# A conditional residual stack on one core: matrices made inside the step, and the last convolution read out in blocks of 32 partitions

## What is computed

```python
# layers 0 and 2 (each with weights of its own)
h = gelu(embedding @ W0 + b0); h = gelu(h @ W1 + b1)
att = softmax(h @ W2 + b2)                                  # 8 weights an example
agg_w = einsum('bk,koi->boi', att, weight[..., 0])          # one 128 x 128 matrix an example
x = x + einsum('boi,bih->boh', agg_w, x) + (att @ bias_k)[:, :, None]
# layers 1 and 3
x = x + conv1d(x, weight, groups=4, padding=4) + (c @ c_weight.T)[:, :, None] + bias[None, :, None]
```

## Time and profile before

| | |
|---|---|
| median of 3 runs | 2982.37 us (2981.94 to 2983.42) |
| profiled execution | 2982.91 us |
| its span, first to last instruction | 2981.1 us |
| PE busy | 2905.9 us (97%) |
| ACT, POOL, DVE busy | 1552.4, 1551.1, 1312.3 us |
| first matmul of layer 0 | at 85.75 us |
| mean granted TensorE clock | 0.985 |

### The profile page before, as it was taken

How to read it: one execution, slowest core, us unless ns; L and a number is a source line. 1 busy time by engine, 2 the same in 40 slices (tenths; PEclk the granted TensorE clock), 3 DMA queues, 4 the chain that set the end, 5 groups by cost and what they waited for, 6 DMA issues and landing times.

```text
span 2981.1 us, 121239 instructions
## 1 busy us (share of the span) xinstructions
PE 2905.9 (97%) x49252; PEld 2885.6 (97%) x49252; DVE 1312.3 (44%) x2142; ACT 1552.4 (52%) x2358; POOL 1551.1 (52%) x1796
## 2 busy tenths in 40 slices
PE   4899999999999999999999999999999999999997
PEld 2799999999999999999999999999999999999996
DVE  5344444444444444444444444444444444444441
ACT  4455555555555555555555555555555555555552
POOL 0455555555555555555555555555555555555552
PEclk7899999999999999999999999999999999999998
DMA  7465665665665665665665655655655656656653
GB/s 312 106 178 157 163 173 157 165 171 158 165 170 158 166 169 158 167 168 158 171 164 158 173 162 158 175 160 158 178 157 159 179 156 161 178 155 162 176 156 110
DMA packets 339978, 493.88 MB, mean 166 GB/s; under 512 B 59624, under 2 KB 190832, under 8 KB 322288
## 3 DMA queue, kind: packets, MB, share of 16 engines
q1 hardware_dynamic: 339952, 493.51, 60.9%
HBM read 208.06 MB, written 150.99 MB: 120 GB/s over the span
## 4 chain that ended last, share of the span: by engine, by line
PE 97%; DMA 1%; DVE 1%; ACT 0%; SPq 0%; issue 0%; POOL 0%; POOLq 0%; DVEq 0%; ACTq 0%
PE ps L317 72%; PE ps L302 24%; DMA mixed<-work 1%; DMA conv_raw<-conv_w 0%; SPq L228 0%; DVE work L558 0%; ACT work L412 0%; DVE y L542 0%; DVE y L587 0%; PE ps L279 0%; DMA work<-mix_b 0%; ACT xp L399 0%; PE ps L251 0%; POOL work L642 0%; DMA m_raw<-mixed 0%
## 5 line engine op out<-in xcount | busy, mean ns | idle before, releaser
L317 PE MATMUL ps<-y,conv_parts 32*128 32x512 f32 x36864 | 2667.9, 390 | 3.2 <-DVE y L587 3.2
L317 PEld LDWEIGHTS ps<-y,conv_parts 32*128 32x128 f32 x36864 | 2547.7, 184 | 9.1 <-DVE y L587 4.1
L587 DVE SCALAR_TENSOR_TENSOR y<-ps,bias,y 128x512 fp32r<-128x512 f32 x1536 | 1085.3, 750 | 1446.9 <-ACT y L438 1440.2
L438 ACT ACTIVATE y<-ps,bias 128x512 fp32r<-128x512 f32 x1536 | 1046.4, 690 | 683.8 <-PE ps L317 646.3
L635 POOL TENSOR_TENSOR xp<-x_t,xp 128x512 fp32r<-128x512 f32 x512 | 647.0, 1300 | 0.0
L302 PE MATMUL ps<-xp,m_parts 32*128 32x512 f32 x6144 | 621.1, 391 | 24.2 <-POOL xp L635 24.2
L628 POOL TENSOR_TENSOR m_parts<-m_raw,m_parts 128x512 fp32r<-128x512 f32 x256 | 331.7, 1296 | 585.5 <-ACT m_parts L444 585.4
L302 PE MATMUL ps<-y,m_parts 32*128 32x512 f32 x6144 | 618.9, 390 | 0.1
L302 PEld LDWEIGHTS ps<-xp,m_parts 32*128 32x128 f32 x6144 | 560.7, 184 | 25.9 <-issue 24.4
L302 PEld LDWEIGHTS ps<-y,m_parts 32*128 32x128 f32 x6144 | 562.2, 183 | 0.7 <-issue 0.5
L624 POOL COPY bias<-bias_table 128x4 f32 (+1 forms) x512 | 102.0, 200 | 816.5 <-DMA work<-work 662.5
(11 more groups left out here) (38 smaller groups left out, 37.3 us busy)
## 6 DMA issues: line engine op xcount, KB each, us to landing
x_t<-x SPq DMA_DIRECT2D x512, 256.0 KB, 5.1
work<-work SPq DMA_DIRECT2D x2048, 64.0 KB, 2.0
out<-work SPq DMA_DIRECT2D x128, 1024.0 KB, 4.8
m_raw<-mixed SPq DMA_DIRECT2D x1024, 64.0 KB, 4.4
mixed<-work SPq DMA_DIRECT2D x8, 2048.0 KB, 7.9
work<-mix_w SPq DMA_DIRECT2D x2, 2048.0 KB, 12.7
conv_raw<-conv_w SPq DMA_DIRECT2D x2, 768.0 KB, 10.8
work<-small SPq DMA_DIRECT2D x1, 852.0 KB
```

The lines of the kernel that those rows point to most:

```text
L317: ins = nc.tensor.matmul(ps[:, 4 + t, :], conv_parts[layer][rows, w, s, :], src[rows, a, p_in, q:q + N], start=(k == 0), stop=(k == CONV - 1))
L438: nc.scalar.activation(dst, src, ACT.Identity, bias=bias[layer][:, k:k + 1]).then_inc(high_set[layer], 1)
L587: nc.vector.scalar_tensor_tensor(out=dst, in0=src, scalar=bias[layer][:, k:k + 1], in1=high.bitcast(fp32), op0=ALU.add, op1=ALU.subtract). ...
```

## The change

The making of the matrices moves from the start into the step. A table of attention weights, repeated on all partitions, is built at the start (`att_table`); the 8 matrices of each mixing layer lie in SBUF with the identity as a ninth (`mix_sb`). For each example and layer a product of 128x1152 elements is made (`prod`), by DVE for layer 0 and by POOL (`scale`) for layer 2, and DVE sums it over the nine to `m_sum`. SP stores this one matrix to `scratch` and loads it back in the layout of `m_raw`.

The last convolution is read by ACT and DVE at once, in pieces of 32 partitions: phases 0 and 1 of each bank by ACT, 2 and 3 by DVE, straight to the channels and times of `o_t`. The 16 shuffle DMAs and the POOL copies are gone. Conv 1 may write a bank when both engines have read their pieces of it. The convolutions go through their shifts input phase by input phase, so that the wait for `low` 2 is one for each phase.

At the start the first weights and x(0) are loaded ahead of the rest, the gelu table is loaded early, and the bias tables are made behind the attention. The last example is stored in four parts.

```diff
+        PIECES = (("act", "act", "dve", "dve"),) * G
+        def pieces(e, g):
+            return [p for p in range(PH) if PIECES[g][p] == e]
+        def out_piece(g, p):
+            return o_t[CG * g:CG * (g + 1), :].rearrange("c (n p) -> c p n", p=PH)[:, p, :]
...
         @block.sync
...
+            def store_matrix(layer, j):
+                sp.wait_ge(summed[layer], j + 1)
+                sp.dma_start(scratch[layer // 2][bass.ds(j, 1)].rearrange("s c o -> (s c) o"), m_sum[layer][:]).then_inc(stored[layer], 16)
+            def load_matrix(layer, j, first):
+                if not first and layer == 0:
+                    sp.wait_ge(m_set[layer], j)
+                sp.wait_ge(stored[layer], 16 * (j + 1))
...
             def step(i, inner):
+                if has(i, inner, -1):
+                    load_matrix(0, i + 1, not inner and i == -1)
                 if has(i, inner, 0):
-                    if inner or i >= 1:
-                        sp.wait_ge(m_set[2], i)
-                    load_matrix(2, i)
-                if has(i, inner, 2):
-                    for g in range(G):
-                        sp.wait_ge(phases_set, nth(i - 2, g))
-                        for p in range(PH):
-                            sp.dma_start(o_ch[CG * g:CG * (g + 1), p, :], o_ph[CG * p:CG * (p + 1), g, :]).then_inc(shuffled[p], 16)
+                    load_matrix(2, i, not inner and i == 0)
+                if has(i, inner, -2):
+                    store_matrix(0, i + 2)
+                if has(i, inner, -1):
+                    store_matrix(2, i + 1)
                 if has(i, inner, -2):
                     sp.wait_ge(x_low_set, 4 * (i + 2))
                     load_x(i + 2)
-                    sp.wait_ge(m_set[0], i + 2)
-                    load_matrix(0, i + 2)
                 if has(i, inner, 2):
-                    sp.wait_ge(in_time_set, 4 * (i - 1))
-                    sp.dma_start(out[i - 2], o_t).then_inc(out_done, 16)
+                    for g in range(G):
+                        if not inner and is_last(i) or g == G - 1:
+                            for e in out_set:
+                                sp.wait_ge(out_set[e], pieces_until(e, i - 2, g))
+                        if not inner and is_last(i):
+                            sp.dma_start(out[i - 2][CG * g:CG * (g + 1)], o_t[CG * g:CG * (g + 1)]).then_inc(out_done, 16)
+                    if inner or not is_last(i):
+                        sp.dma_start(out[i - 2], o_t[:]).then_inc(out_done, 16)
...
         @block.tensor
...
                 def free1(g):
                     if before:
-                        pe.wait_ge(phases_set, nth(i - 2, g))
+                        out_read(i - 2, g)
...
         @block.scalar
...
                 if before:
                     for g in range(G):
                         act.wait_ge(mm[3], nth(i - 2, g))
                         if g == 0:
                             act.wait_ge(bias_set[3], i - 1)
                             if inner or i > 2:
-                                for p in range(PH):
-                                    act.wait_ge(shuffled[p], 16 * G * (i - 2))
-                        nc.scalar.activation(o_ph[:, g, :], ps[:, 4 + g, :], ACT.Identity,
-                                             bias=bias[3][:, g:g + 1]).then_inc(phases_set, 1)
+                                act.wait_ge(out_done, 16 * (i - 2))
+                        for p in pieces("act", g):
+                            rows = slice(CG * p, CG * (p + 1))
+                            nc.scalar.activation(out_piece(g, p), ps[rows, 4 + g, :], ACT.Identity,
+                                                 bias=bias[3][rows, g:g + 1]).then_inc(out_set["act"], 1)
...
         @block.vector
...
+            def matrix(layer, j, first):
+                l = layer // 2
+                if layer == 0:
...
+                    nc.vector.tensor_tensor(prod[layer][:], mix_sb[layer][:],
+                                            att_table[:, bass.ds(j, 1), l, :].broadcast_to([128, C, K + 1]),
+                                            ALU.mult).then_inc(scaled[layer], 1)
+                dve.wait_ge(scaled[layer], j + 1)
+                if not first:
+                    dve.wait_ge(stored[layer], 16 * j)
+                nc.vector.tensor_reduce(m_sum[layer][:], prod[layer][:], AX_X, ALU.add).then_inc(summed[layer], 1)
...
+                if has(i, inner, 2):
+                    for g in range(G):
+                        dve.wait_ge(mm[3], nth(i - 2, g))
+                        if g == 0:
+                            dve.wait_ge(bias_set[3], i - 1)
+                            if inner or i > 2:
+                                dve.wait_ge(out_done, 16 * (i - 2))
+                        for p in pieces("dve", g):
+                            rows = slice(CG * p, CG * (p + 1))
+                            nc.vector.tensor_scalar(out_piece(g, p), ps[rows, 4 + g, :], bias[3][rows, g:g + 1], None,
+                                                    ALU.add).then_inc(out_set["dve"], 1)
                 if last:
                     for p in range(PH):
                         low(2, i - 1, p, y3[:, LOW, p, 1:N + 1], ps[:, p, :], y3[:, HIGH, p, 1:N + 1])
+                if has(i, inner, -2):
+                    matrix(0, i + 2, False)
+                if has(i, inner, -1):
+                    matrix(2, i + 1, not inner and i == -1)
```

More of the change, by code:

```diff
@@ L73, in build_cond_resid, with part_of @@
-        room = work[:, 3, :]
-        stage = [work[:, k, :] for k in range(5)]
-        SLOT = (0, 1, 3, 2, 3, 4, 2, 4)
-        taken = {"room": 0, "room_r": 0}
-        def part_of(name, shape):
+        room = sb("room", [128, small.shape[1]])
+        taken = [0]
+        def part_of(shape):
             width = 1
@@ L217, in _ @@
-            load_matrix(0, 0)
+            def store_matrix(layer, j):
[5 more added lines that the diff above has]
+                sp.wait_ge(stored[layer], 16 * (j + 1))
+                if not first and layer == 2:
+                    sp.wait_ge(m_set[layer], j)
+                for q in range(G):
+                    sp.dma_start(m_raw[layer][CG * q:CG * (q + 1)],
+                                 scratch[layer // 2][bass.ds(j, 1)].rearrange("s (g c) o -> (s c) g o", g=G)).then_inc(m_in[layer], 16)
@@ L281, in _ @@
-            for m in range(QB):
-                mixed_out(2 * Q - 1, m)
-            pe.wait_ge(zeros_set, 1)
-            pe.wait_ge(conv_set, 2)
+                nc.tensor.matmul(ps[:, 2 + l, 0:B], mix_b_sb[:, l, :], att_t[:, l, :], start=True, stop=True).then_inc(mix_b_mm, 1)
+            pe.wait_ge(ctx_in, 16)
+            pe.wait_ge(table_act, 1)
+            pe.wait_ge(table_dve, 1)
+            for l in range(2):
+                for g in range(G):
+                    last = nc.tensor.matmul(ps[:, 6 + l, g * B:(g + 1) * B], ctx_w_sb[:, l, g, :], emb_sb, start=True, stop=True)
+                last.then_inc(ctx_mm, 1)
@@ L582, in _ @@
-            last.then_inc(zeros_set, 1)
-            def low(layer, j, k, dst, src, high):
-                dve.wait_ge(high_set[layer], nth(j, k))
-                nc.vector.scalar_tensor_tensor(out=dst, in0=src, scalar=bias[layer][:, k:k + 1],
-                                               in1=high.bitcast(fp32), op0=ALU.add, op1=ALU.subtract).then_inc(low_set[layer], 1)
             def x_high(j, first):
@@ L596, in x_high, with conv_identity @@
                     nc.vector.tensor_copy(xp[:, HIGH, g, :], x_t[:, g, :]).then_inc(x_high_set, 1)
+            def conv_identity(layer):
+                dve.wait_ge(conv_in[layer], 16)
+                shifts = conv_raw[layer][:].rearrange("p (s m) -> p s m", s=SHIFTS)
+                for p in range(PH):
+                    own = shifts[:, PH + p, CG * p:CG * (p + 1)]
+                    last = nc.vector.tensor_tensor(own, own, ident_g, ALU.add)
+                last.then_inc(conv_ident_set, 1)
@@ new lines, in _, with low @@
+            conv_identity(1)
+            att_rows(0)
+            matrix(0, 0, True)
+            for l in range(2):
+                dve.wait_ge(att_t_mm, l + 1)
+                nc.vector.tensor_copy(att_t[:, l, :], ps[0:K, l, 0:B]).then_inc(att_t_set, 1)
+            att_rows(1)
+            conv_low_part(1)
+            def low(layer, j, k, dst, src, high):
+                dve.wait_ge(high_set[layer], nth(j, k))
+                nc.vector.scalar_tensor_tensor(out=dst, in0=src, scalar=bias[layer][:, k % WIDTH[layer]:k % WIDTH[layer] + 1],
+                                               in1=high.bitcast(fp32), op0=ALU.add, op1=ALU.subtract).then_inc(low_set[layer], 1)
@@ L667, in step @@
                     set_bias(2, i)
-                if before:
-                    in_time(i - 2)
+                if now:
+                    matrix_low(2, i)
+            pool.wait_ge(first_in, 32)
+            x_low(0)
+            pool.wait_ge(mix_b_read, 2)
```

(3 more changed lines are left out.)

448 lines of the change are left out of this document (191 added, 257 removed).

## The result

The changed kernel takes **3823.32 us** (median of 4 runs, 3821.88 to 3828.56) against 2982.15 us for the kernel before (4 runs, 2981.89 to 2983.42): a ratio of 1.2823, 95% interval 1.2801 to 1.2845. The prediction was 3250 us with a range of 2990 to 3430: the sign was right, the size far too small, and the time lies above the range.

A forecast was written before the change was run, and what follows sets the result against it. PE's matmuls were taken to bound the kernel at 22.3 us a step. From 2982.9 us, 59 (start) and 13 (tail) come off, leaving 2911; 124 steps each 2.72 us longer add 337, giving 3250 us, range 2990 to 3430.

The forecast's parts named there:

- What bounds the kernel: Main loop before the change: PE's 384 matmuls set each step at 22.30 us; other engines' work is free within deadlines.
- the window of 4.4 us: Time from the first read of conv 3's banks until conv 1 needs the last bank free: 4.4 us a step.
- The price of a piece: Readout of conv 3: pieces 0.61 us apart on ACT, 0.70 on DVE; eight take 5.0 and 5.7 us.
- start and tail: Before and behind the loop: first mix-0 matmul at 27 us saves 59 us, a shorter end saves 13.
- Overlap of neighbours: Readout pieces on DVE: queued pieces overlap and come 0.70 us apart, against 0.82 whole.
- the rival's mechanism: DVE's readout: each piece changing its partition block waits for the one before; step 25.85 us, 3351 us in all, chance 0.22.
- The loop through SP: SP's queue: x, out and the layer-0 matrix wait behind the sums' stores, making a step 25.0 us; chance 0.45.
- M: End of the second sum, the last instruction of DVE's step, from which the later times are counted.
- Lanes: Readout: 32 partitions cost a quarter, eight pieces take some 2.4 us, 2936 us in all; chance 0.12.
- Only the evacuation waits: Readout: transfers arrive in time, pieces overrun the bank deadline by 0.6 to 1.3 us a step, 3035 us; chance 0.13.
- More at once: DVE: product held 1.3 us behind POOL's `matrix_low`, on top of held pieces; step 27 us, about 3500 us; chance 0.08.

The follow-up runs named there:

- e4: Changed kernel with the load of x and the store of out put ahead of the stores of the sums in SP's queue: 3650.75 us.
- e7: Kernel before with only the readout replaced by the sixteen pieces on ACT and DVE, matrices still made ahead of the loop: 3722.23 us.
- the last corner of the table: Changed kernel with pieces writing dense columns and each engine keeping to one block of 32 partitions: 3176.92 us.
- after: The changed kernel itself, as profiled after the change: 3823.32 us.
- e5: Changed kernel with pieces writing dense columns, and x and out ahead of the sums' stores in SP's queue: 3137.50 us.
- e6d: Matrices made in the step, before's readout, sums behind the casts, their stores between the shuffles, start reordered on DVE, ACT and POOL: 2931.48 us.
- e6b: Matrices made in the step as in the changed kernel, before's readout, x ahead of the sums' stores, DVE's sums behind its casts: 3111.65 us.

## Why the prediction was wrong, point by point

- **What bounds the kernel, and the window of 4.4 us: right.** A window that long, filled with 9.5 us, gives 22.3 + 5.1 = 27.4 us a step; e4 and e7 measured 27.1 in steps at full clock.
- **The price of a piece: the step that failed.** ACT 0.61 and DVE 0.70 apart were predicted, 1.19 and 1.17 came. Eight pieces to the first layer-2 read took 9.53 us instead of 4.88: 4.65 us in each of 124 steps are 577 us, and the result was 573 above the forecast. That the two agree so closely is partly luck: start and tail fell 21 us short of their terms, and the rest of the loop gave some 24 back. The rows chosen were of reads and casts written column by column. The term asked how 32 partitions and PSUM reads are priced and never what the new write pattern, one column in four, costs. The row of the same operation, L505, could have raised the doubt: it too writes with a step (64 bytes), and comes every 0.31 us for 128 columns, 2.4 ns a column with the fixed part of an instruction in it; the prediction used it, but priced the other 384 columns at 1.04 ns. They cost (1134 - 418)/384 = 1.86. A rule was also there: the Trainium skill, "Advanced Engine Details and Errata", "SBUF Cachelines", says that accesses that stay in one 16-byte line run at full speed and that a different line at each access is penalised. A step of four fp32 columns is just that. The trace agrees (1163 against 679 ns, 1157 against 687); the page gives no price.
- **Overlap of neighbours: the rival's mechanism was right, its reach too small.** The prediction gave 0.22 to pieces held because their block changes, and only on DVE, by the Trainium skill's model ("VectorE: DVE Perf Modes", "Two Vector instructions with no wait between them"). The runs agree with the model on DVE: 0.78 against 0.66 apart, dense. ACT behaves alike (0.70 against 0.57), of which that section doesn't speak. It isn't the bulk: from the last corner of the table it adds 135 us dense, the step of the write 373, both together 646.
- **The loop through SP: right in its terms.** x M+0.8 (0.65 predicted), casts M+8.6 (8.1), matrix cast M+11.8 (11.8), pieces M+12.3 (12.4), sums 4.0 (4.2), the four casts beside POOL 3.6 us (3.9). But it isn't what decides: taking it out alone saves 173 us (e4), and without it the readout alone costs 740 (e7). In after both ways round take some 29.3 us: the loop by itself, since most groups of pieces start right behind ACT's cast (ACT's pieces wait for PE in 42 of 128 cases), and PE's by 9.5 + 17.6 and what the lower clock adds.
- **The clock: not in the prediction.** It reckoned PE's waits as lost time alone. In the two steps of after shown above, matmuls behind the wait run at the lower level, 26 us of busy time instead of 22.3. With the shorter waits of e5 the clock stays at 1.00 in nearly every step.
- **Start and tail: too good.** 59 us were predicted for the first mix 0 and 51.7 came. The prediction's own terms put it at 26.3 (24 + 6.9 - 1.3 - 3.3), given as 27; it came at 34.08. The load of the matrix went at 25.93 and not at 20.7 (24 - 3.3), because DVE's casts and identity stand ahead of the table: in e6d, where they don't, the first product starts at 14.34 instead of 21.61. From the load it took 8.15 us instead of 5.6, since POOL's low part stood behind the copies that wait for the context matmuls (which the prediction had taken off this path), an identity and a product. At the first read of conv 3 42.5 were left. The tail gave 8.4 instead of 13: the last pieces take 9.35 us, not 2 beside the matmuls.
- **The other rivals.** *Lanes* is wrong: 679 ns with 32 partitions, 687 with 128. *Only the evacuation waits* had the right place (e7), with a piece at half its price. *More at once* was nearest by its figure, but not for its reason: the pieces do wait for one another, yet the product, which it let stand still for 1.3 us, took 1365 ns, near the 1.32 forecast.

## What to carry to other kernels

Price an instruction by how it writes as well as by what it reads: one that scatters its columns needs a row of a scattered write, and splitting a read over blocks of partitions buys nothing where the time goes with columns, and loses the overlap. When a change makes two bundled moves, price them one by one; here the matrices in the step were worth 51 us and the readout cost 740. And a transfer that must wait for a late result is put in its queue where that result is long there, not where the next one is due.

## What the runs showed that was not expected

- A write to every fourth fp32 column costs 0.94 ns a column more on ACT (484 ns in 512; 470 with 128 partitions) and 0.75 on DVE (382, with 32 partitions). A longer step costs about the same: a copy of 512 columns that writes the table in steps of 72 bytes (L408, L507 in after) takes 1116 ns on ACT and 1106 on DVE.
- A read from PSUM with the same step costs nothing on ACT: the four layer-0 reads of ACT, which take every fourth column and write them side by side, come out at 681 to 694 ns (means in the loop of after), layer 1's at 688.
- ACT's neighbours lose their overlap, some 0.13 us each when dense, if the block of 32 partitions changes; whole banks of 128 partitions keep it.
- A 64 KB store behind 1 MB in flight takes 5.2 us to land (e6b, median), 1.6 in after where nothing is ahead of it.
